# Local attention in six layers: the mask added by VectorE, the maximum taken off by GpSimd, and the second pair of query/key products moved ahead of the output product

## The chip, the cores and the metric

The kernel runs on one core of a Trainium2 chip. The metric is the device time of one execution in microseconds (us), measured outside the profiler; the profile is a separate look at one execution with its own time. The engines are TensorE (PE for matmuls, PEld for its weight loads), VectorE (DVE), ScalarE (ACT), GpSimd (POOL) and SyncE (SP), which issues the transfers. Each engine works through its own instructions in the order in which they stand, and semaphores tie the engines together.

## The reference, cut to what matters

The program has four parts and a last normalisation. The change is in the fourth, a network of six layers, each with a local attention and a feed-forward part, on 16 sequences of 256 tokens with 128 features. The attention has 16 heads of 64 features. A window is 32 tokens, and each token sees its own window and the one before, as far as the mask lets it.

```python
def local_attention(q, k, v):
    w = WINDOW                       # 32
    nw = n // w
    bk2, bv2 = (look(bk), look(bv))  # the window before, and the own one: 64 keys
    mask = (it < jb) | (it > jb + w) | (jb == -1)
    sim = jnp.einsum('bhwie,bhwje->bhwij', bq, bk2) * QK_SCALE
    sim = jnp.where(mask, -jnp.finfo(sim.dtype).max, sim)
    attn = jax.nn.softmax(sim, -1)
    out = jnp.einsum('bhwij,bhwje->bhwie', attn, bv2)
    return out.reshape(b, h, n, d)

def attn_layer(x, Wqkv, qs, ksc, Wo):
    q, k, v = jnp.split(x @ Wqkv, 3, -1)          # heads split off each
    q = l2norm(q) * qs
    k = l2norm(k) * ksc
    q = q * cos * scale + rotate_half(q) * sin * scale
    k = k * cos * inv + rotate_half(k) * sin * inv
    out = local_attention(q, k, v)
    return out @ Wo

for i in range(6):
    x = attn_layer(shift_tokens(x), ...) + x
    x = ffn_layer(shift_tokens(x), ...) + x
```

## The kernel before

**Tiling.** All layers run in `l1_network`, one loop over six layers. In a layer the 16 sequences follow each other, written out one by one; `N` counts them. A sequence has 256 tokens, so two blocks of 128, `j` = 0 and 1. What one call of `attention` does for one sequence has two halves, one for each `j`, and the four compute engines each have their own `attention` function that writes out that engine's part.

**A pipeline over three sequences.** In half `j` of sequence `N` the engines work at three sequences at once:

- for `N+1`, the query/key products `project_qk(N+1, 4j..4j+3)`, four of 128x512, called c below; each is squared by ScalarE (`square`) and multiplied by the rotary tables by VectorE (`rotate`), and the two halves of the rotation are added by GpSimd (`add`). VectorE sums the squares per head (`sum_squares`), ScalarE makes inverse norms of them (`inverse_norms`), GpSimd multiplies by these (`norm`), TensorE transposes the result (`turn_qk`) and ScalarE copies it (`copy_qk`). The value products are `project_v`;
- for `N`, the mask products, the scores, the softmax, the transposes of the weights (`turn_weights`) and their copies (`copy_weights`), and the weighted sums of the values (`weigh`, half a step later);
- for `N-1` (or the block before), the transposes of the normed output (`turn_output`), their copies (`copy_output`), the output product (`output`), and its sum with the residual in `X` (`add_attention`, on VectorE).

A sequence that is first in its layer has no `N-1` part (`prev` is false), and the last has no `N+1` part (`nxt` is false).

**The softmax before.** `masks` writes the mask into the two score banks `pS` with one bfloat16 product of an identity with the mask for each; `scores` accumulates onto it with 64 small products (two passes each in float32, so 128 in the trace). VectorE takes the maxima of `pS` (`maxima`), subtracts them into `E`, ScalarE exponentiates `E` (`exps`), VectorE sums it (`sum_exps`) and makes reciprocals.

**Two banks in turn.** All other products and transposes of a half go in turn into the banks 2 and 3 of the PSUM tile `pp`, in the order of the list `SHARED`. A use waits until the use before the last one, which had the same bank, has been read. In half `j` the order is: two value products, two `turn_output`, the output product (called y), then four `turn_qk`. So the output product takes the bank of the first `turn_output`, the first `turn_qk` that of the second `turn_output`, and the second `turn_qk` that of the output product: it waits for `add_attention`, which reads that bank and increments `s_x`. The query/key products have the banks 0 and 1, in turn by c.

```python
    def bank(*use):
        kind, c, d = at[use][1]
        freed(kind, c, N + d)
        return at[use][0]
```

```python
    elif kind == "y":
        after(pe, s_x, 2 * N + c + 1)
```

There is no scheduler: the order on each engine is the order of the calls in its `attention` function.

## Time and profile before

| | us |
|---|---|
| median of 3 runs | 4645.14 (4640.55 to 4652.28) |
| the profiled execution's own time | 4643.52 |
| its span, first to last instruction | 4641.7 |
| PE busy | 4093.0 (88%) |
| DVE busy | 3365.0 (72%) |
| ACT busy | 2392.2 (52%) |
| POOL busy | 2163.8 (47%) |

The profiled execution lies 1.6 us under the median, and its span 1.8 us under its own time. The busy shares are means over stages that differ: the six layers lie between about 1,090 and 4,600 us, and in the attention of a layer the pattern repeats with each sequence, so one sequence in the trace tells of nearly all of that stage. The places in the trace that matter here are named by their time from the span's start.

### The profile page before, as it was taken

The page shows a single profiled execution, that of the slowest core. Times are in us where ns is not written, and L with a number is a line of the kernel's source. Part 1 is how long each engine was busy: PE and PEld are TensorE (multiplying, and loading weights), DVE is VectorE, ACT ScalarE, POOL GpSimd, SP SyncE. Part 2 cuts the span into 40 slices and gives each one's busy share as a digit, 9 for nine tenths or more (in the row PEclk, how much of TensorE's full clock was granted, in tenths as well). Part 3 has the DMA queues.
Part 4 walks back from the last instruction along what each step waited for, and adds up shares of the span by engine and source line. Part 5 has one row for each costly group of instructions (what it writes and reads, how often), then busy time and mean ns, then how long its engine had stood idle before and what let it go on. Part 6 is the DMA issues. An engine that isn't in the chain of part 4 may idle for free. (4 is left out here: it accounts for less than half of the span.)

```text
span 4641.7 us, 175927 instructions
## 1 busy us (share of the span) xinstructions
PE 4093.0 (88%) x68914; PEld 2806.2 (60%) x68915; DVE 3365.0 (72%) x7216; ACT 2392.2 (52%) x5386; POOL 2163.8 (47%) x2301
## 2 busy tenths in 40 slices
PE   7999749576999889998899989999889998899995
PEld 4566416454666656666566665666656666566663
DVE  4777450576888778887788877888778887788876
ACT  4666423123666546665366653666536665366651
POOL 2444300103566436664366643666436664366651
PEclk9999769798999999999999999999999999999998
DMA  1000003003333223332233322333223332223221
GB/s 41 5 5 3 1 21 98 8 0 85 66 71 66 47 65 70 66 68 49 65 70 64 71 48 65 67 67 69 50 65 66 68 68 51 64 64 71 62 57 43
DMA packets 478517, 249.52 MB, mean 54 GB/s; under 512 B 65782, under 2 KB 472516, under 8 KB 476740
## 3 DMA queue, kind: packets, MB, share of 16 engines
q1 hardware_dynamic: 477764, 238.93, 23.1%
q8 instruction: 539, 8.83, 0.8%
q14 instruction: 214, 1.75, 0.1%
HBM read 35.40 MB, written 4.19 MB: 9 GB/s over the span
## 5 line engine op out<-in xcount | busy, mean ns | idle before, releaser
L1921 POOL TENSOR_TENSOR n_pre<-n_tt 128x512 f32<-128x512 f32 x768 | 970.9, 1275 | 886.1 <-DVE n_tt L2394 886.1
L2394 DVE TENSOR_TENSOR n_tt<-n_pp,n_rot 128x1024 f32<-128x1024 f32 x768 | 922.2, 1220 | 378.6 <-ACT n_sq L2255 378.5
L1942 POOL TENSOR_TENSOR n_pre<-n_pre,n_rn 128x512 f32<-128x512 f32 x768 | 776.6, 1042 | 284.4 <-ACT n_rn L2263 284.4
L2021 PE MATMUL n_pp<-n_wqkv,n_xT 128*128 128x512 f32 x1536 | 787.9, 615 | 10.7 <-ACT n_xT L2250 10.4
L2255 ACT ACTIVATE n_sq<-n_pp 128x512 f32<-128x512 f32 x768 | 459.1, 598 | 595.5 <-PE n_pp L2021 584.7
L2401 DVE TENSOR_REDUCE n_ss<-n_sq 128x8 f32<-128x512 f32 x768 | 518.8, 676 | 0.0
L2275 ACT COPY n_qkT<-n_pp 128x512 f32<-128x512 f32 x768 | 436.6, 594 | 136.6 <-PE n_pp L2037 136.1
L2037 PE MATMUL n_pp<-ident,n_pre 128*128 128x128 f32 x3072 | 433.2, 274 | 19.7 <-POOL n_pre L1942 14.5
L2051 PE MATMUL n_pp<-n_wo,n_OT 128*128 128x128 f32 x3072 | 398.7, 283 | 58.1 <-ACT n_OT L2281 57.1
L2037 PEld LDWEIGHTS n_pp<-ident,n_pre 128*128 128x128 f32 x3072 | 360.3, 142 | 129.1 <-issue 125.4
L2051 PEld LDWEIGHTS n_pp<-n_wo,n_OT 128*128 128x128 f32 x3072 | 361.4, 193 | 103.6 <-ACT n_OT L2281 101.2
L2281 ACT COPY n_OT<-n_pp 128x512 f32<-128x512 f32 x384 | 206.5, 589 | 339.4 <-PE n_pp L2044 339.4
L2028 PE MATMUL n_pp<-n_wqkv,n_xT 128*128 128x512 f32 x768 | 366.3, 597 | 0.0
L2071 PEld LDWEIGHTS n_pS<-n_qkT 64*32 64x32 f32 x24576 | 254.6, 105 | 162.0 <-issue 161.8
L301 POOL TENSOR_TENSOR a_E<-a_E,a_ri 128x256 f32<-128x256 f32 (+1 forms) x256 | 211.4, 826 | 291.8 <-DVE a_ri L536 291.3
L2021 PEld LDWEIGHTS n_pp<-n_wqkv,n_xT 128*128 128x128 f32 x1536 | 250.7, 192 | 139.0 <-issue 111.3
L2096 PE MATMUL n_pW<-n_V,n_ET 64*32 64x64 f32 x12288 | 295.8, 225 | 28.5 <-issue 28.5
L2408 DVE TENSOR_REDUCE n_nm<-n_pS 128x8 f32<-128x512 f32 x384 | 247.3, 686 | 97.8 <-PE n_pS L2071 97.8
L2096 PEld LDWEIGHTS n_pW<-n_Vx,n_ET 64*32 64x32 f32 x12288 | 249.7, 105 | 106.7 <-issue 106.7
L2071 PE MATMUL n_pS<-n_qkT 64*32 64x64 f32 (+1 forms) x24576 | 287.7, 222 | 23.5 <-issue 23.5
L2096 PE MATMUL n_pW<-n_Vx,n_ET 64*32 64x64 f32 x12288 | 290.1, 225 | 16.5 <-issue 11.6
L2431 DVE TENSOR_TENSOR n_On<-n_pW,n_ri 128x512 f32<-128x512 f32 x384 | 246.2, 683 | 43.4 <-PE n_pW L2096 41.7
(246 smaller groups left out, 7016.9 us busy)
## 6 DMA issues: line engine op xcount, KB each, us to landing
n_V<-n_Vn SPq DMA_DIRECT2D x768, 128.0 KB, 2.6
n_Vx<-n_Vn SPq DMA_DIRECT2D x384, 128.0 KB, 2.5
n_Vx<-n_Vn SPq DMA_DIRECT2D x576, 64.0 KB, 2.2
n_wqkv<-in_L_ffn_Wqkv SPq DMA_DIRECT2D x6, 1536.0 KB, 6.7
e_w<-in_L_ffn_w SPq DMA_DIRECT2D x32, 256.0 KB, 3.0
n_fxs<-X SPq DMA_DIRECT2D x48, 127.0 KB
m_Y<-e_ye SPq DMA_DIRECT2D x64, 64.0 KB, 2.1
n_wo<-in_L_ffn_Wo SPq DMA_DIRECT2D x6, 512.0 KB, 7.3
```

The source lines that it names most:

```text
L1921: nc.gpsimd.tensor_tensor(d, s[0], s[1][:, :, ::-1, :], ALU.add).then_inc(s_add, 1)
L1942: nc.gpsimd.tensor_tensor(d, d, bcast(rn[:, j, t, 8 * half:8 * half + 8], 2, D), ALU.mult).then_inc(s_kn, 1)
L2021: nc.tensor.matmul(pp[:, c % 2, :], xT[:, j * P:(j + 1) * P], wqkv[:, t * I + 512 * half:t * I + 512 * half + 512], start=True, stop=True) ...
L2028: nc.tensor.matmul(pp[:, bank, :], xT[:, j * P:(j + 1) * P], wqkv[:, 2 * I + 512 * half:2 * I + 512 * half + 512], start=True, stop=True). ...
L2037: last = nc.tensor.transpose(pp[:, bank, g * P:(g + 1) * P], pre[:, j, t, o:o + P], ident[:, :])
L2051: last = nc.tensor.matmul(pp[:, bank, 0:C], OT[:, j, k % 2, k // 2, :], wo[:, k, :], start=(k == 0), stop=(k == I // P - 1))
L2071: last = nc.tensor.matmul(pS[W * w:W * w + W, e, i * 2 * W + o:(i + 1) * 2 * W], qkT[r:r + D, 0, i, q:q + W], qkT[r:r + D, 1, i, lo:q + W] ...
L2096: last = nc.tensor.matmul(pW[W * w:W * w + W, f, o:o + D], ET[r:r + D, e, c, W * w:W * w + W], v[r:r + D, u, m, o:o + D], start=True, stop ...
L2255: nc.scalar.activation(sq[:, c % 2, :], pp[:, c % 2, :], ACT.Square).then_inc(s_sq, 1)
L2275: nc.scalar.copy(qkT[:, t, 4 * half:4 * half + 4, j * P:(j + 1) * P], pp[:, bank, :].rearrange("p (g q) -> p g q", g=4)).then_inc(s_qkT, 1)
L2394: nc.vector.tensor_tensor(tt[:, c % 4, :, :].rearrange("p s (h d) -> p s h d", d=D), bcast(pp[:, c % 2, :].rearrange("p (h d) -> p h d", d ...
L2401: nc.vector.tensor_reduce(ss[:, j, t, 8 * half:8 * half + 8], sq[:, c % 2, :].rearrange("p (h d) -> p h d", d=D), AX.X, ALU.add).then_inc( ...
```

## The change

The parts of the change, all in the attention of the six layers:

- `masks` and its bfloat16 identity go. The scores start their banks themselves (`start=True`). For the first window of a sequence, which has no window before it, the product now takes its own 32 keys twice, so that all 64 places hold something; the mask puts the first 32 out.
- VectorE adds the mask while it moves the scores from `pS` to `E` (`mask_scores`), and takes the maxima of `E`.
- GpSimd takes the maxima off (`take_maximum`), in place in `E`, after the four `norm` of the half and ahead of its four `add`.
- TensorE makes the second pair of query/key products right after `turn_output`, ahead of the output product; before, they stood between and behind the `turn_qk`. The second `turn_qk` stands ahead of `turn_weights`.
- ScalarE squares the second pair ahead of `exps` (there are four buffers of squares now); VectorE rotates both ahead of `sum_exps`, and `sum_exps` stands ahead of `add_attention`.

```diff
             def attention(N, u, b, prev, nxt, nxt2):        # GpSimd
...
+                for j in range(2):
+                    if nxt or not j:
+                        clamp_squares(N + j, 1 - j)
+                        for r in range(4):
+                            norm(N + j, 1 - j, r)
+                    take_maximum(N, j)
+                    if nxt:
+                        for c in range(4 * j, 4 * j + 4):
+                            add(N + 1, c)
+                    elif not j:
+                        ff_start(layer[0])
...
+            def take_maximum(N, j):
+                for e in range(2):
+                    after(pool, s_max, 4 * N + 2 * j + e + 1)
+                    x = E[:, e, :].rearrange("p (i s) -> p i s", s=2 * W)
+                    nc.gpsimd.tensor_tensor(x, x, bcast(nm[:, j, e, :], 2, 2 * W), ALU.subtract
+                                            ).then_inc(s_sub, 1)
...
-                    masks(N, j)                              # TensorE
                     if j == 1:
+                        held(pe, s_held)
                         weigh(u, 0)
...
+                    after(pe, s_masked, 4 * N + 2 * j)
...
+                            if j == 0 and w == 0:
+                                keys = bcast(qkT[r:r + D, 1, i, 0:W], 1, 2)
+                            else:
+                                keys = qkT[r:r + D, 1, i, q - W:q + W]
...
+                    if nxt:
+                        project_qk(N + 1, 4 * j + 2)
+                        project_qk(N + 1, 4 * j + 3)
                     if prev:
                         output(N - 1, j, bank("y", j, -1))
                     d = j
                     if nxt or not d:
                         turn_qk(N + d, 4 - 4 * j, bank("turn", 4 - 4 * j, d))
+                        turn_qk(N + d, 5 - 4 * j, bank("turn", 5 - 4 * j, d))
                     turn_weights(N, j)
-                    if nxt or not d:
-                        turn_qk(N + d, 5 - 4 * j, bank("turn", 5 - 4 * j, d))
-                    if nxt:
-                        project_qk(N + 1, 4 * j + 2)
...
+            def mask_scores(N, j):                           # VectorE
+                after(dve, s_S, 4 * N + 2 * j + 2)
                 after(dve, s_ETp, 4 * N + 2 * j)
                 for e in range(2):
...
+                                            bcast(win[:, j, :], 1, 8), ALU.add).then_inc(s_masked, 1)
+                for e in range(2):
+                    after(dve, s_masked, 4 * N + 2 * j + e + 1)
+                    nc.vector.tensor_reduce(nm[:, j, e, :], E[:, e, :].rearrange("p (i s) -> p i s", s=2 * W),
+                                            AX.X, ALU.max).then_inc(s_max, 1)
...
-                    maxima(N, j)
+                    mask_scores(N, j)
                     if nxt:
                         sum_squares(N + 1, 4 * j + 1)
+                        rotate(N + 1, 4 * j + 2)
+                        rotate(N + 1, 4 * j + 3)
+                    sum_exps(N, j)
                     if prev:
                         add_attention(N - 1, b - 1, j, at["y", j, -1][0])
-                    sum_exps(N, j)
                     if nxt:
-                        for c in (4 * j + 2, 4 * j + 3):
-                            rotate(N + 1, c)
-                            sum_squares(N + 1, c)
+                        sum_squares(N + 1, 4 * j + 2)
+                        sum_squares(N + 1, 4 * j + 3)
```

**On TensorE**, in the half `j` = 0 of a sequence inside a layer, from the output product to the last `turn_qk`. L2051 is the output product, L2037 `turn_qk`, L2083 `turn_weights`, L2021 a query/key product. Before:

```order
L2051 MATMUL n_pp<-n_wo,n_OT 128x128 [waits n_outT_copied]
L2051 MATMUL n_pp<-n_wo,n_OT 128x128 x7
L2037 MATMUL n_pp<-ident,n_pre 128x128 [waits n_qk_normed,n_outT_copied]
L2037 MATMUL n_pp<-ident,n_pre 128x128 x3
L2083 MATMUL n_pW<-ident,n_E 128x128 [waits n_exped,n_output_normed]
...
L2037 MATMUL n_pp<-ident,n_pre 128x128 [waits n_qk_normed,n_attention_added]
L2037 MATMUL n_pp<-ident,n_pre 128x128 x3
L1809 REGISTER_ALU
L2021 MATMUL n_pp<-n_wqkv,n_xT 128x512 [waits n_xT_copied,n_rotary_products]
L2037 MATMUL n_pp<-ident,n_pre 128x128 [waits n_qk_normed,n_qkT_copied]
```

Now, with the same steps at L2054, L2040, L2078 and L2024:

```order
L2024 MATMUL n_pp<-n_wqkv,n_xT 128x512 [waits n_xT_copied,n_rotary_products]
L2054 MATMUL n_pp<-n_wo,n_OT 128x128 [waits n_outT_copied]
L2054 MATMUL n_pp<-n_wo,n_OT 128x128 x7
L2040 MATMUL n_pp<-ident,n_pre 128x128 [waits n_qk_normed,n_outT_copied]
L2040 MATMUL n_pp<-ident,n_pre 128x128 x3
L1807 ISA
L2040 MATMUL n_pp<-ident,n_pre 128x128 [waits n_qk_normed,n_attention_added]
L2040 MATMUL n_pp<-ident,n_pre 128x128 x3
L2078 MATMUL n_pW<-ident,n_E 128x128 [waits n_exped,n_output_normed]
```

The `turn_qk` that waits for `add_attention` stood behind `turn_weights`; it stands ahead of it now, right behind the output product and the first `turn_qk`.

**On VectorE**, in the same half, from the scores on. Before, with L2408 the maxima, L2413 the subtraction, L2401 a sum of squares, L2438 `add_attention`, L2420 and L2423 `sum_exps`, L2394 `rotate`:

```order
L2408 TENSOR_REDUCE n_nm<-n_pS 128x8 [waits n_scored]
L2408 TENSOR_REDUCE n_nm<-n_pS 128x8
L1809 REGISTER_ALU [waits n_weights_turned]
L2413 TENSOR_TENSOR n_E<-n_pS,n_nm 128x512 [waits n_maxed] x2
L2401 TENSOR_REDUCE n_ss<-n_sq 128x8 [waits n_norms_made]
L2438 TENSOR_TENSOR X<-n_pp,X 128x128 [waits n_y_made]
L2420 TENSOR_REDUCE n_rs<-n_E 128x8 [waits n_exped] x2
L2423 RECIPROCAL n_ri<-n_rs 128x16 [waits n_exps_summed]
L1809 REGISTER_ALU [waits n_rotary_added]
L2394 TENSOR_TENSOR n_tt<-n_pp,n_rot 128x1024 [waits n_squared]
```

Now, with the mask at L2400, the maxima at L2405 and `add_attention` at L2429:

```order
L2400 TENSOR_TENSOR n_E<-n_pS,n_win 128x512 [waits n_weights_turned,n_scored]
L2400 TENSOR_TENSOR n_E<-n_pS,n_win 128x512
L1807 REGISTER_ALU
L2405 TENSOR_REDUCE n_nm<-n_E 128x8 [waits n_scores_masked] x2
L2392 TENSOR_REDUCE n_ss<-n_sq 128x8 [waits n_norms_made]
L1807 REGISTER_ALU [waits n_rotary_added]
L2385 TENSOR_TENSOR n_tt<-n_pp,n_rot 128x1024 [waits n_squared]
L1807 REGISTER_ALU [waits n_rotary_added]
L2385 TENSOR_TENSOR n_tt<-n_pp,n_rot 128x1024 [waits n_squared]
L2411 TENSOR_REDUCE n_rs<-n_E 128x8 [waits n_exped] x2
L2414 RECIPROCAL n_ri<-n_rs 128x16 [waits n_exps_summed]
L2429 TENSOR_TENSOR X<-n_pp,X 128x128 [waits n_y_made]
```

`add_attention` was the second step behind the softmax pair; now the two rotations, both sums of exponentials and the reciprocal stand ahead of it.

## Rows read from the trace of the kernel before

**Rows 1.** Busy time in a stretch of one sequence (us): engines, granted PE clock, DMA.

```profile
1302.33:1332.33 30.00, 29.05 (x640) 20.55 (x639) 24.89 (x36) 18.97 (x39) 18.95 (x20) 1.00 0.32 69
```

**Rows 2.** Timeline of PE in that sequence: start us, us, line, tiles [idle before].

```profile
1302.33 0.25 PE L2096 MATMUL n_pW<-n_Vx,n_ET 64*32 64x64 f32 x2
...
1303.74 1.98 PE L2021 MATMUL n_pp<-n_wqkv,n_xT 128*128 128x512 f32 x4
1305.56 1.88 PE L2028 MATMUL n_pp<-n_wqkv,n_xT 128*128 128x512 f32 x4
1307.37 1.46 PE L2071 MATMUL n_pS<-n_qkT 64*32 64x32 f32 x128
1308.76 1.09 PE L2044 MATMUL n_pp<-ident,n_On 128*128 128x128 f32 x8
1310.15 2.05 PE L2051 MATMUL n_pp<-n_wo,n_OT 128*128 128x128 f32 x16 [0.29 <-ACT n_OT L2281]
1312.04 0.60 PE L2037 MATMUL n_pp<-ident,n_pre 128*128 128x128 f32 x4
1312.47 1.04 PE L2083 MATMUL n_pW<-ident,n_E 128*128 128x128 f32 x8
1313.35 0.60 PE L2037 MATMUL n_pp<-ident,n_pre 128*128 128x128 f32 x4
1313.79 1.02 PE L2021 MATMUL n_pp<-n_wqkv,n_xT 128*128 128x512 f32 x2
1314.65 1.04 PE L2037 MATMUL n_pp<-ident,n_pre 128*128 128x128 f32 x8
...
1316.38 0.59 PE L2059 MATMUL n_pS<-n_win,n_eye 128*128 128x512 bf16 x2
1316.90 0.25 PE L2096 MATMUL n_pW<-n_Vx,n_ET 64*32 64x64 f32 x2
...
1321.95 1.48 PE L2071 MATMUL n_pS<-n_qkT 64*32 64x64 f32 x128
...
1330.65 0.43 PE L2014 MATMUL n_pp<-ident,n_xs 128*128 128x128 f32 x2 [0.37 <-ACT n_qkT L2275]
```

**Rows 3.** Timeline of DVE in the first half of that sequence.

```profile
1305.56 2.35 DVE L2394 TENSOR_TENSOR n_tt<-n_pp,n_rot 128x1024 f32<-128x1024 f32 x2
1307.83 0.67 DVE L2401 TENSOR_REDUCE n_ss<-n_sq 128x8 f32<-128x512 f32 x1
1308.90 1.29 DVE L2408 TENSOR_REDUCE n_nm<-n_pS 128x8 f32<-128x512 f32 x2 [0.40 <-PE n_pS L2071]
1310.10 1.28 DVE L2413 TENSOR_TENSOR n_E<-n_pS,n_nm 128x512 f32<-128x512 f32 x2
1311.30 0.68 DVE L2401 TENSOR_REDUCE n_ss<-n_sq 128x8 f32<-128x512 f32 x1
1312.24 0.29 DVE L2438 TENSOR_TENSOR X<-n_pp,X 128x128 f32<-128x128 f32 x1 [0.27 <-PE n_pp L2051]
1312.45 1.27 DVE L2420 TENSOR_REDUCE n_rs<-n_E 128x8 f32<-128x512 f32 x2
1313.75 0.25 DVE L2423 RECIPROCAL n_ri<-n_rs 128x16 f32<-128x16 f32 x1
```

**Rows 4.** Timelines of ACT and POOL in that half.

```profile
1310.82 1.23 ACT L2286 ACTIVATE n_E<-n_E 128x512 f32<-128x512 f32 x2 [0.23 <-DVE n_E L2413]
...
1313.21 1.08 ACT L2291 COPY n_ET<-n_pW 128x512 f32<-128x512 f32 x2
...
1306.88 4.05 POOL L1942 TENSOR_TENSOR n_pre<-n_pre,n_rn 128x512 f32<-128x512 f32 x4 [1.08 <-ACT n_rn L2263]
```

**Rows 5.** Busy time in stretches that begin with a PE gap; one at half clock.

```profile
1126.70:1133.90 7.20, 5.03 (x66) 3.36 (x68) 5.83 (x11) 5.33 (x10) 4.51 (x5) 1.00 0.68 144
...
4528.00:4535.20 7.20, 4.98 (x11) 2.26 (x12) 3.49 (x8) 1.62 (x3) 0.00 (x0) 0.76 0.05 11
```

**Rows 6.** The same view, of the granted clock's fall after one such gap.

```profile
1595.20:1598.59 3.39, 3.39 (x17) 3.07 (x16) 2.03 (x4) 2.31 (x4) 0.00 (x0) 0.50 0.10 22
1592.00:1595.00 3.00, 0.98 (x45) 0.89 (x45) 0.50 (x2) 0.00 (x0) 0.00 (x0) 1.00 0.08 18
```

More of the change, by code:

```diff
@@ L1961, in attention @@
                     stage(N + 2, u, b + 2)
-                clamp_squares(N, 1)
-                for r in range(4):
-                    norm(N, 1, r)
-                if nxt:
-                    for c in range(4):
-                        add(N + 1, c)
-                    clamp_squares(N + 1, 0)
-                    for r in range(4):
-                        norm(N + 1, 0, r)
-                    for c in range(4, 8):
-                        add(N + 1, c)
-                else:
-                    ff_start(layer[0])
+                for j in range(2):
[9 more added lines that the diff above has]
+                        ff_start(layer[0])
             def ff_stage(M, g, p):
@@ L2053, in output @@
                 last.then_inc(s_y, 1)
-            def masks(N, j):
-                after(pe, s_sub, 4 * N + 2 * j)
-                for e in range(2):
-                    nc.tensor.matmul(pS[:, e, :].rearrange("p (i s) -> p i s", s=2 * W), eye[:, :],
-                                     bcast(win[:, j, :], 1, 8), start=True, stop=False, skip_group_check=True)
             def scores(j):
@@ L2137, in attention @@
                         weights_ready(pairs[0], N - 1, 1 - u, 1)
-                    if not nxt:
-                        after(pe, s_qkT, 8 * N + 4 * j + 4)
-                    masks(N, j)
                     if j == 1:
+                        held(pe, s_held)
                         weigh(u, 0)
                     elif prev:
+                        held(pe, s_held)
                         weigh(1 - u, 1)
@@ L2147, in attention @@
                         project_qk(N + 1, 4 * j + 1)
-                        after(pe, s_qkT, 8 * N + 4 * j + 4)
+                    after(pe, s_qkT, 8 * N + 4 * j + 4)
+                    after(pe, s_masked, 4 * N + 2 * j)
+                    if nxt:
                         project_v(N + 1, 2 * j, bank("v", 2 * j, 1))
                         project_v(N + 1, 2 * j + 1, bank("v", 2 * j + 1, 1))
+                    else:
+                        held(pe, s_held)
                     scores(j)
@@ L2252, in square @@
             def square(N, c):
-                after(act, s_ss, 8 * N + c - 1)
+                after(act, s_ss, 8 * N + c - 3)
                 after(act, s_qk, 8 * N + c + 1)
-                nc.scalar.activation(sq[:, c % 2, :], pp[:, c % 2, :], ACT.Square).then_inc(s_sq, 1)
+                nc.scalar.activation(sq[:, c % 4, :], pp[:, c % 2, :], ACT.Square).then_inc(s_sq, 1)
             def inverse_norms(N, j):
```

45 lines of the change are left out of this document (13 added, 32 removed).

## The prediction

> **What bounds the kernel now.** I read the whole span in stretches of 100 us first; inside the attention of a layer they all look alike, so the next view is one sequence, 30.00 us long [rows 1]: PE is busy for 29.05 of it at a clock of 1.00, DVE for 24.89, ACT and POOL for 19 each. Then PE's timeline of that sequence [rows 2]. It runs without a break but for three short stops: 0.29 us ahead of the output product in each half (the bank of the first `turn_output` is not yet copied) and 0.37 us ahead of `turn_x`. So here PE is the bound, and whatever PE no longer does or no longer waits for shortens the sequence, until a wait of PE takes its place. A half runs from one start of `weigh` to the next: 1302.33 to 1316.90, 14.57 us, and 15.43 us for the other, which holds `turn_x`. There are 16 sequences in each of six layers; 14 of the 16 have a neighbour on both sides.
>
> **The change part by part.** I take the half from 1302.33 and price each step by the distance from its start to the next start in [rows 2], since PE overlaps the end of one product with the next.
>
> *What goes.* The mask products: 1316.38 to 1316.90, 0.52 us a half, all on the path. The stop of 0.29 us ahead of the output product: with two query/key products in front of it (0.86 us each, 1313.79 to 1314.65), ScalarE has 1.7 us more to copy, so it goes. That is 0.81 us a half, 1.62 a sequence, if nothing else becomes late. The products for the first window grow from 32 to 64 columns; the scores of the other half, which are all of 64, take 1.48 against 1.46 us, so 0.02. The new `held` rows on PE are sequencer rows without work; I bound them by 0 and 0.1 us a half and take 0.
>
> *What moves work off or onto VectorE.* Two additions of the mask take the place of two subtractions, from the same PSUM tile and of the same shape (two in 1.20 us, 1310.10 to 1311.30 [rows 3]); the maxima read SBUF now (before two in 1.20 us from PSUM, 1308.90 to 1310.10; `sum_exps` reads E and takes 1.27 for two against 1.29). So nothing.
>
> *GpSimd's two subtractions.* The nearest row is the four `norm`: in place, float32, 128x512, second operand broadcast over 64: 4.05 us, 1.0 each [rows 4]. In the new half GpSimd has finished `norm` about 2.2 us behind the end of the scores (1310.93 against 1308.76), when the first maxima are there too; the subtractions end at 3.2 and 4.2, the exponentials (0.6 each) at 3.9 and 4.9. Their first reader is `turn_weights` or `sum_exps`, which by the next paragraph come at 6.0 or later. So they are hidden, with 1 us of room; at 1.28 us each still; from about 1.6 us each they would show.
>
> *The wait that decides.* The second `turn_qk` goes into the bank of the output product and therefore waits for `add_attention`. Before it stood behind `turn_weights` and started at 1313.35, 0.8 us after `add_attention` had ended (1312.24 + 0.29 [rows 3]). Now PE reaches it earlier, and VectorE reaches `add_attention` later. I count from the end of the scores, 1308.76.
>
> - PE: two `turn_output` 0.88 (eight transposes, priced like the eight of `turn_weights`, 1312.47 to 1313.35, since their own row holds the stop), two query/key products 1.72, output product 1.89, first `turn_qk` 0.43: PE stands at the second `turn_qk` at **4.92**.
> - VectorE starts 0.14 behind (1308.90), then masks 1.20, maxima 1.20, a sum of squares 0.60, two rotations 2.27 (1305.56 to 1307.83), two sums of exponentials with the step to the reciprocal 1.30 (1312.45 to 1313.75), reciprocal 0.25, `add_attention` 0.29: **7.25**, and some 0.05 until PE sees it (ScalarE saw a subtraction 0.04 after its end, 1310.82). Nothing in this chain waits: squares, products and exponentials are all earlier.
>
> So PE waits 7.30 - 4.92 = **2.4 us in each half**, where nothing waited; as PE's last transposes end some 0.17 us after their issue (1312.04 + 0.60 against 1312.47), the visible gap is about 2.2. What is queued behind it on PE is the rest of the half: `turn_qk`, `turn_weights` and, behind their copies, `weigh`, and with it the next half's norms. All engines then run with room to spare.
>
> *The new half.* `weigh` 1.41, two query/key products 1.82, two value products 1.81, scores 1.39, then 7.30 to the end of the wait, then `turn_qk` 0.44, `turn_weights` 0.88, two `turn_qk` 0.87 and about 0.1 until `weigh` has its copies (ScalarE copies the second `turn_qk` ahead of the two weight copies, 1.08 [rows 4]): **16.0** against 14.57. In the half with `turn_x`, PE waits about 0.6 us for the copy that frees its bank and then turns for 0.27 (1330.65 on): **16.95** against 15.43. A sequence takes 33.0 instead of 30.0. The first sequence of a layer has no output product to wait for and gains the masks and some of the stop, about 0.5; the last has no rotations, yet has to wait for GpSimd in both halves; I bound it by 0 and 3 and take 2. A layer: 14 x 3.0 - 0.5 + 2 = 43.5; six: **+261 us**.
>
> *The clock.* Gaps of this size on PE are in the trace at the ends and starts of layers: 20 gaps of 2.17 to 2.40 us behind 1,100 us, of which the first and the last stand in [rows 5]. After nine, as after the first, the granted clock stayed at 1.00; after eleven, as after the last, it fell to half, the lower of its two levels (1.2 instead of 2.4 GHz), which makes the mean of these 7 us 0.76. [rows 6] show one fall: PE busy for 0.98 of 3 us, then 3.39 us at 0.50. In 3.4 us at half clock PE does the work of 1.7; some 0.5 of that falls into waits for copies (those ahead of `weigh` and `turn_x`), so I take 1.2 us a fall, between 0.7 and 1.7. Of 29 waits a layer I let 16 (11 in 20) be followed by a fall: 16 x 6 x 1.2 = **+115 us**. The Trainium skill ("TensorE: Matmul & The Clock Gate", section "HAM oscillation — how this bites in real kernels") tells of a kernel whose matmuls wait for a transfer at every tile and whose clock is throttled anew at every one of them. By that, all 174 waits would bring a fall; the nine gaps without one speak against it.
>
> *Sum.* 4643.5 (the profiled execution, 1.6 under the median) + 261 + 115 = 5020.
>
> **The rivals.**
>
> *A, the clock holds.* All waits as above, no fall: 4643.5 + 261 = 4905. For it: nine of 20 gaps. Against it: eleven, and here the gap comes at ever other places in time, so that some must be like these.
>
> *B, a fall at every wait.* 174 falls at 1.2 are 209, so 5113; at 1.7 they are 296, so 5200. For it: all eleven gaps with a fall are of 2.2 us or more, as long as the one expected here. Against it: three of that length had none.
>
> *C, faster: the wait doesn't bind.* Then 0.81 us goes from each half and PE stays the bound: a sequence takes 28.4, of which DVE's 24.89 still fit; 15 x 6 x 1.62 = 146, so 4498. It decides at 4.92 us behind the scores: `add_attention` would have to end by then, so the two rotations (2.27) would have to stand behind it, or the bank be another. Against it: the new order shows `n_attention_added` at that very row, and the rotations ahead of it on VectorE. For it there would have to be a step that I misread.
>
> *D, it evens out.* If the wait were 0.8 us, gain and loss would cancel: 4645. VectorE's chain would have to be 1.6 us shorter than its rows say; nothing points there.
>
> **How the numbers follow.** Forecast (waits of 2.4 us, some falls) 0.78; A 0.07; B 0.06; C 0.06; D 0.03. The predicted time is the forecast's, 5020. Its unknowns: 0.7 to 1.7 us a fall on a third to two thirds of the waits gives 40 to 200, and the last sequence of a layer ±6 to ±12 over six layers, so 4940 to 5115; A lies at 4905. The range from 4900 to 5105 leaves out C, D, most of B and the forecast's ends. What a measurement of this kernel can tell from no change is about 0.3%, 14 us. Slower by more than that: forecast, A, B, 0.91; within it: D, 0.03; faster: C, 0.06.
>
> **What would show each step right or wrong.** In the profile after: no L2059 rows and no idle time ahead of the output product; a wait of the second `turn_qk` for DVE's X of about 2.2 us, in some 29 halves a layer; `take_maximum` at 1.0 us with its exponentials done before `sum_exps` begins; PE's busy share in the attention near 86%; a sequence of 33 us where the clock holds; and a granted clock under 1.00 in most stretches of 100 us. The prediction is wrong if PE shows no wait for X, if DVE's steps behind the scores take less than 6 us until X is added, or if the halves differ in length without a change of the clock.

## The result, and the profile after

The changed kernel takes 5137.71 us (median of 4 runs, 5127.55 to 5158.42) against 4647.47 us (4640.55 to 4652.28) for the kernel before in the same runs: a ratio of 1.1062, 95% interval 1.1019 to 1.1104, so 490 us slower. The forecast was 5020, the range 4900 to 5105. The direction and the wait that makes most of the loss came as forecast; the time is 33 us above the range.

From the page after: the span, busy time and share of the engines, one DMA queue (packets, MB, share), and two groups of instructions (busy us, mean ns of one, idle time ahead and what ended it).

```profile
span 5156.6 us, 176394 instructions
PE 4199.3 (81%) x68530; PEld 2940.4 (57%) x68531; DVE 3336.3 (65%) x7214; ACT 2428.0 (47%) x5386; POOL 2536.6 (49%) x2685
q8 instruction: 539, 8.83, 0.7%
L2040 PE MATMUL n_pp<-ident,n_pre 128*128 128x128 f32 x3072 | 504.5, 304 | 382.8 <-DVE X L2429 367.8
L1961 POOL TENSOR_TENSOR n_E<-n_E,n_nm 128x512 f32<-128x512 f32 x384 | 392.5, 1043 | 76.8 <-DVE n_nm L2405 73.2
```

PE is now busy for 81% of the span. The waits of PE say why: 174 waits of up to 2.2 us of `turn_qk` (L2040) for the residual's sum on DVE (L2429), 29 a layer, where the kernel before had none.

```profile
PE n_pp L2040 <- DVE X L2429: 367.8, 174, 2.2
PE n_pW L2091 <- issue: 123.1, 89, 2.7
```

The second row has a sister in the view of the waits of the kernel before, where `weigh` is L2096; it stands in none of the rows ahead of the prediction, and that is where the prediction fell short:

```profile
PE n_pW L2096 <- issue: 40.1, 65, 1.2
```

One half of a sequence on PE's timeline after (start, us, line; idle time and its releaser in brackets), to be laid beside [rows 2]. It is the half with `turn_x` (L2017), from one start of `weigh` to the next, 1302.86 to 1319.74:

```profile
1309.31 1.09 PE L2047 MATMUL n_pp<-ident,n_On 128*128 128x128 f32 x8
1310.24 1.88 PE L2024 MATMUL n_pp<-n_wqkv,n_xT 128*128 128x512 f32 x4
1311.96 1.95 PE L2054 MATMUL n_pp<-n_wo,n_OT 128*128 128x128 f32 x16
1313.74 0.60 PE L2040 MATMUL n_pp<-ident,n_pre 128*128 128x128 f32 x4
1316.45 0.66 PE L2040 MATMUL n_pp<-ident,n_pre 128*128 128x128 f32 x4 [2.10 <-DVE X L2429]
1316.94 1.04 PE L2078 MATMUL n_pW<-ident,n_E 128*128 128x128 f32 x8
1317.81 1.04 PE L2040 MATMUL n_pp<-ident,n_pre 128*128 128x128 f32 x8
1319.38 0.43 PE L2017 MATMUL n_pp<-ident,n_xs 128*128 128x128 f32 x2 [0.53 <-ACT n_qkT L2270]
1319.74 0.25 PE L2091 MATMUL n_pW<-n_Vx,n_ET 64*32 64x64 f32 x2
...
1322.95 0.24 PE L2091 MATMUL n_pW<-n_Vx,n_ET 64*32 64x64 f32 x2 [1.79 <-issue]
1323.19 1.98 PE L2024 MATMUL n_pp<-n_wqkv,n_xT 128*128 128x512 f32 x4
```

There are two breaks. The first, of 2.10 us, is the forecast wait. The forecast has no term for the second: `weigh` starts at 1319.74, runs for about a microsecond and stops; what ends the stop is "issue", so no semaphore of the profile. "Stop" below is such a break in the dense products of `weigh`; its length is counted from the start of the last product ahead of it to the start of the next, here 1320.93 to 1322.95. DVE's timeline in the same half, the chain that PE waits for, beside [rows 3]:

```profile
1309.44 1.29 DVE L2400 TENSOR_TENSOR n_E<-n_pS,n_win 128x512 f32<-128x512 f32 x2 [0.44 <-PE n_pS L2068]
1310.65 1.27 DVE L2405 TENSOR_REDUCE n_nm<-n_E 128x8 f32<-128x512 f32 x2
1311.84 0.68 DVE L2392 TENSOR_REDUCE n_ss<-n_sq 128x8 f32<-128x512 f32 x1
1312.43 2.35 DVE L2385 TENSOR_TENSOR n_tt<-n_pp,n_rot 128x1024 f32<-128x1024 f32 x2
1314.69 1.27 DVE L2411 TENSOR_REDUCE n_rs<-n_E 128x8 f32<-128x512 f32 x2
1315.99 0.25 DVE L2414 RECIPROCAL n_ri<-n_rs 128x16 f32<-128x16 f32 x1
1316.16 0.23 DVE L2429 TENSOR_TENSOR X<-n_pp,X 128x128 f32<-128x128 f32 x1
```

And the windows (PE, PEld, DVE, ACT, POOL busy, granted clock, DMA share, GB/s): a half with nothing but the wait, the next half with a stop and a fall of the clock, the 3 us ahead of that fall, and the fall (a stretch at a granted clock of 0.50).

```profile
1302.86:1319.74 16.88, 14.25 (x318) 10.28 (x318) 12.33 (x18) 9.91 (x20) 11.57 (x12) 1.00 0.26 57
1319.74:1339.45 19.71, 15.73 (x317) 11.84 (x316) 12.33 (x18) 9.54 (x19) 11.26 (x11) 0.91 0.26 56
1332.70:1335.70 3.00, 0.81 (x8) 0.57 (x6) 2.97 (x6) 1.01 (x2) 3.00 (x3) 1.00 0.75 157
1335.70:1339.11 3.41, 3.41 (x18) 3.41 (x17) 0.88 (x2) 1.82 (x4) 1.93 (x3) 0.50 0.11 29
```

**Where the 490 us are.** I cut both traces at the starts of `weigh` and took the 168 halves that have a neighbour on both sides (28 a layer). Their mean went from 15.27 to 17.99 us: +457. A sequence without a stop or the start of a fall went from 29.96 to 33.45 us (the means of its two halves, 15.39 + 14.58 and 17.09 + 16.36): 84 x 3.49 = +293. 90 of the halves hold a fall of the clock, none did before; each adds 1.23 us (0.36 us for each us at half clock, as a line through all halves gives it, times 3.41): +111. The stops inside `weigh` sum to 103.8 against 45.7 us: +58. That makes 462, 5 too many, since these parts overlap a little. Outside these halves, the first half of each layer took 16.5 us more in all, and the ends and starts of the layers 18: +34. (The two profiled executions lie 515 us apart, more than the medians; the other 24 us lie ahead of the layers, where the change does nothing.)

The +293 is not the wait alone. In the changed kernel PE also stops on "issue" in the scores and right behind them, in 21 of the 168 halves for 18.6 us in all; before, in none of these halves (the twelve of L2071 lie at the ends of the layers). The waits after, and in the third row those of the scores before:

```profile
PE n_pS L2068 <- issue: 33.0, 24, 2.4
PE n_pp L2047 <- issue: 10.7, 11, 1.7
PE n_pS L2071 <- issue: 23.5, 12, 2.4
```

Without these halves, and without those into which a fall of the half before reaches, a sequence takes 33.11 us.

Of the 92 falls (two halves hold two), 74 begin between 0.2 us before and 1.2 us after the end of the wait for X; the other 18 begin 2 to 5 us behind a start of `weigh`, right behind a stop.

**What a stop is.** Ahead of each of them a transfer of 16 KB on the instruction queue q8 begins, 2.3 to 2.7 us before PE goes on in the changed kernel. The DMA view of the stretch 1320.00 to 1321.50 (busy tenths in 40 slices, and the one queue that moved anything) shows it for the stop above:

```profile
DMA  0000000000000009000000000000000000000000
q8 instruction: 1, 0.02, 3.9%
```

The sixteenth slice begins at 1320.56, 0.8 us behind the start of `weigh`; PE goes on at 1322.95, 2.4 us later. In all kernels of this study PE goes on 2.40 to 2.56 us after such a transfer began (mean of each kernel's stops) and the stop begins 1.1 us behind the start of `weigh`; what differs is when the transfer begins. There are 40 to 61 stops in the 168 halves of each kernel, 53 in the one before, where they were 0.83 us long. A transfer alone makes no stop: each half has two or three of them, and most halves have no stop. In the changed kernel all 48 stops of these halves fall on the same eight halves of every layer. That PE waits for these transfers is read from their times; no run takes the transfers away.

### The profile page after: what moved, and what is told of

Read it like the earlier page. It is cut to its first block and busy times, and to the rows that moved or that the text cites. A ratio compares the mean times of both kernels' runs of the same rounds, so it can differ in the third digit from the quotient of the medians.

```text
span 5156.6 us, 176394 instructions
## 1 busy us (share of the span) xinstructions
PE 4199.3 (81%) x68530; PEld 2940.4 (57%) x68531; DVE 3336.3 (65%) x7214; ACT 2428.0 (47%) x5386; POOL 2536.6 (49%) x2685
## 5 line engine op out<-in xcount | busy, mean ns | idle before, releaser
L1919 POOL TENSOR_TENSOR n_pre<-n_tt 128x512 f32<-128x512 f32 x768 | 954.2, 1275 | 135.3 <-DVE n_tt L2385 135.3
L2385 DVE TENSOR_TENSOR n_tt<-n_pp,n_rot 128x1024 f32<-128x1024 f32 x768 | 906.9, 1218 | 110.5 <-ACT n_sq L2250 110.1
L2040 PE MATMUL n_pp<-ident,n_pre 128*128 128x128 f32 x3072 | 504.5, 304 | 382.8 <-DVE X L2429 367.8
L2024 PE MATMUL n_pp<-n_wqkv,n_xT 128*128 128x512 f32 x1536 | 788.7, 636 | 12.7 <-ACT n_xT L2245 12.7
L2040 PEld LDWEIGHTS n_pp<-ident,n_pre 128*128 128x128 f32 x3072 | 404.8, 158 | 442.4 <-DVE X L2429 409.2
L2392 DVE TENSOR_REDUCE n_ss<-n_sq 128x8 f32<-128x512 f32 x768 | 503.0, 674 | 0.0
L2054 PEld LDWEIGHTS n_pp<-n_wo,n_OT 128*128 128x128 f32 x3072 | 374.4, 193 | 98.6 <-issue 79.1
L1961 POOL TENSOR_TENSOR n_E<-n_E,n_nm 128x512 f32<-128x512 f32 x384 | 392.5, 1043 | 76.8 <-DVE n_nm L2405 73.2
L2024 PEld LDWEIGHTS n_pp<-n_wqkv,n_xT 128*128 128x128 f32 x1536 | 274.8, 199 | 236.5 <-issue 212.2
L2054 PE MATMUL n_pp<-n_wo,n_OT 128*128 128x128 f32 x3072 | 379.6, 277 | 13.7 <-ACT n_OT L2276 13.6
L2400 DVE TENSOR_TENSOR n_E<-n_pS,n_win 128x512 f32<-128x512 f32 x384 | 247.5, 686 | 138.3 <-PE n_pS L2068 138.3
L2068 PE MATMUL n_pS<-n_qkT 64*32 64x64 f32 x24576 | 291.5, 226 | 33.0 <-issue 33.0
```

Source lines behind the costliest of these rows:

```text
L1919: nc.gpsimd.tensor_tensor(d, s[0], s[1][:, :, ::-1, :], ALU.add).then_inc(s_add, 1)
L1961: nc.gpsimd.tensor_tensor(x, x, bcast(nm[:, j, e, :], 2, 2 * W), ALU.subtract).then_inc(s_sub, 1)
L2024: nc.tensor.matmul(pp[:, c % 2, :], xT[:, j * P:(j + 1) * P], wqkv[:, t * I + 512 * half:t * I + 512 * half + 512], start=True, stop=True) ...
L2040: last = nc.tensor.transpose(pp[:, bank, g * P:(g + 1) * P], pre[:, j, t, o:o + P], ident[:, :])
L2054: last = nc.tensor.matmul(pp[:, bank, 0:C], OT[:, j, k % 2, k // 2, :], wo[:, k, :], start=(k == 0), stop=(k == I // P - 1))
L2068: last = nc.tensor.matmul(pS[W * w:W * w + W, e, i * 2 * W:(i + 1) * 2 * W], qkT[r:r + D, 0, i, q:q + W], keys, start=True, stop=True)
```

## The experiments

All ratios are to the kernel before in the same runs, with 95% intervals. Four things had to be told apart: the wait for the residual's sum, the clock, the stops inside `weigh`, and the share of the mask's move.

### The wait: the sum between the rotations

```diff
                         rotate(N + 1, 4 * j + 2)
+                    if prev:
+                        add_attention(N - 1, b - 1, j, at["y", j, -1][0])
+                    if nxt:
                         rotate(N + 1, 4 * j + 3)
                     sum_exps(N, j)
-                    if prev:
-                        add_attention(N - 1, b - 1, j, at["y", j, -1][0])
```

> The changed kernel with one step moved on VectorE: the sum with the residual (add_attention) stands between the two rotations, not behind both and behind the sums of exponentials. If the wait of the second turn_qk for that sum is what the change costs (theory W): the output product ends 4.5 us behind the scores, the sum 0.3 later, PE reaches that turn_qk at 4.9, so the wait and most falls of the clock go; 0.8 us a half against the kernel before remain as a gain, less the longer stops inside weigh (some 75 us in the changed kernel's trace), so 4540 to 4640. If the subtraction on GpSimd lengthens the softmax (theory G): the time stays near the changed kernel's, above 4900. If the stops inside weigh bring the falls of the clock (theory S): the wait goes, the stops of 2.2 us stay, with some 50 falls of 1.2 us: 4600 to 4700.

4703.54 us, ratio 1.0111 (1.0077 to 1.0145). Moving one call of 0.23 us on DVE takes some 440 us off the changed kernel (1.1062 - 1.0111, times 4650). The time lies above the 4540 to 4640 that theory W gave. The wait for X is gone from PE's waits, and what now stands first is the stop:

```profile
PE n_pW L2091 <- issue: 141.5, 104, 2.7
```

A sequence without stop or fall takes 29.01 us, 0.95 less than before (the parts that go promised 1.6). And still the kernel is 1.1% slower than before: the stops sum to 117 us in the 168 halves, and 23 falls come with them, all in halves with a stop.

### The stops: slow work ahead of `weigh`

The changed kernel, with one product of 128x512 (0.87 us), whose result nothing reads, right ahead of `weigh`:

```diff
+                    if j == 1 or prev:
+                        held(pe, s_held)
+                        after(pe, s_masked, 4 * N + 2 * j)
+                        nc.tensor.matmul(pS[:, 0, :], ident[:, :], wo[:, 0:4, :].rearrange("p k n -> p (k n)"),
+                                         start=True, stop=True)
                     if j == 1:
-                        held(pe, s_held)
                         weigh(u, 0)
                     elif prev:
-                        held(pe, s_held)
                         weigh(1 - u, 1)
```

> The changed kernel with one product more in each half, right ahead of weigh: a float32 product of the identity with 512 columns of Wo into a score bank that the scores overwrite; its result is not used, and it is about 0.87 us of PE. In the changed kernel weigh stops about 64 times for 2.1 us on average in its last quarter, in the kernel before, with a product and the masks (1.4 us) ahead of weigh, for 0.8 us. If PE's instructions come too late there (theory S) and slow work ahead of weigh gives them time: the stops shrink by about 0.9 us, to 1.3, 75 us in place of 132; falls of the clock become rarer, perhaps by a third (40 us). Against that stand 190 products, 165 us if all are on the path. So 5137 + 165 - 57 - 40 = 5200, and 5160 to 5250. If the stops have another cause, they keep their 2.1 us: 5300. The wait for the residual's sum stays at 2.1 us in both.

5189.79 us, ratio 1.1154 (1.1113 to 1.1195). Added work of 0.87 us in each of 186 halves would be 162 us; the kernel grew by 43. The wait for X is untouched, the stops went from a mean of 2.22 us to 1.17, and the falls from 90 to 63:

```profile
PE n_pp L2040 <- DVE X L2432: 369.7, 174, 2.2
PE n_pW L2091 <- issue: 49.3, 49, 1.7
```

A sequence without stop or fall grew by 1.65 us, so the added work is on the path, and most of what it costs comes back from stops and falls. The length of a stop hangs on what PE does right ahead of `weigh`.

### The two parts of the change alone

First the mask and GpSimd's part alone, with the products, squares, rotations and transposes in the old order:

```diff
-                    if nxt:
-                        project_qk(N + 1, 4 * j + 2)
-                        project_qk(N + 1, 4 * j + 3)
                     if prev:
                         output(N - 1, j, bank("y", j, -1))
...
+                    turn_weights(N, j)
+                    if nxt or not d:
                         turn_qk(N + d, 5 - 4 * j, bank("turn", 5 - 4 * j, d))
-                    turn_weights(N, j)
+                    if nxt:
+                        project_qk(N + 1, 4 * j + 2)
...
+                    if nxt:
+                        project_qk(N + 1, 4 * j + 3)
```

> One part alone: the mask added by VectorE and the maximum taken off by GpSimd as in the changed kernel; the second pair of query/key products, its squares, rotations, the second turn_qk and add_attention stand where the kernel before has them. Theory W: no wait for the residual's sum. But turn_weights, 3.5 us behind the scores, now comes ahead of the exponentials, which end 3.9 and 4.9 us behind the scores because of GpSimd: some 1.1 us of wait a half in two pieces, less 0.5 for the masks: 31.1 us a sequence against 30.0, and with longer stops in weigh 4760 to 4840. Theory G: the subtraction costs as much as the whole change, above 5000. If the mask part is a plain gain (its chain hidden): 4550.

4790.75 us, ratio 1.0293 (1.0257 to 1.033). No fall in the 168 halves; the stops have a mean of 1.32 us, with the product (0.86) ahead of `weigh` but not the masks (0.52). Most of the loss is a wait of `turn_weights` for the exponentials, which in this order come later than PE, behind GpSimd's two subtractions (276 times, 12 before). The second row, ahead of the output product, stood at 57.1 us before:

```profile
PE n_pW L2078 <- ACT n_E L2283: 118.0, 276, 3.4
PE n_pp L2054 <- ACT n_OT L2278: 62.4, 183, 1.4
```

Then the moves alone, with the mask products and DVE's subtraction as before (the diff is that of the change without `mask_scores`, `take_maximum` and the scores' own start):

> The other part alone: the second pair of query/key products ahead of the output product, squares, rotations, both first turn_qk ahead of turn_weights, the sums of exponentials ahead of add_attention, all as in the changed kernel; mask products on PE, maxima and subtraction on VectorE as before. Theory W: VectorE's chain ahead of add_attention has the same length as in the changed kernel, 7.25 us, so the turn_qk waits its 2.1 us in every half; with the masks (0.5 us a half) a sequence takes 34.1 us: 4985 without a fall of the clock, up to 5150 with a fall at every second wait. The stops in weigh, with 0.5 us of mask products ahead, lie between those of the kernel before and of the changed one. Theory G: about the kernel before or faster, 4550 to 4660.

5101.36 us, ratio 1.0963 (1.0926 to 1.1001). The wait is there at nearly its full size, 70 falls with it, and with the masks alone ahead of `weigh` the stops have 1.56 us:

```profile
PE n_pp L2037 <- DVE X L2434: 354.7, 170, 2.1
```

The moves thus hold most of the loss.

### The clock: the wait filled with work

Two products more in each half, read by nothing, right where PE waits for X:

```diff
                         turn_qk(N + d, 4 - 4 * j, bank("turn", 4 - 4 * j, d))
+                        if prev:
+                            after(pe, s_masked, 4 * N + 2 * j + 2)
+                            for e in range(2):
+                                nc.tensor.matmul(pS[:, e, :], ident[:, :],
+                                                 wo[:, 4 * e:4 * e + 4, :].rearrange("p k n -> p (k n)"),
+                                                 start=True, stop=True)
                         turn_qk(N + d, 5 - 4 * j, bank("turn", 5 - 4 * j, d))
```

> The changed kernel with two products more in each half, whose results nothing reads (identity by 512 columns of the output weights, 0.87 us each, into pS), right ahead of the second turn_qk, where TensorE waits 2.2 us for add_attention. They take 1.74 us of that wait and change nothing that the wait is for. If the clock falls of the changed kernel come from this gap: they drop from 90 to under 30 and the time by 70 to 110 us, to 5030 to 5070 us, while the wait for VectorE's add_attention drops from 367.8 to some 70 us without any gain of its own. If the falls come from the stops inside weigh: they stay at 80 to 90 and the time at 5120 to 5180 us.

5039.68 us, ratio 1.0862 (1.0824 to 1.09): with 1.74 us of work added to each half the kernel is faster than the changed one, by 0.0200 x 4634 = 93 us. The falls in the 168 halves go from 90 to 25, all of these in halves with a stop, 3 to 6 us behind the start of `weigh`; 65 falls of 1.23 us are 80 us, and the stops gave another 11 us (93.2 against 103.8). A sequence without stop or fall still takes 33.40 us, since X is as late as before:

```profile
PE n_pp L2040 <- DVE X L2435: 70.1, 165, 0.6
```

This run parts the two prices of the wait: the lost time itself, and the clock that an idle PE loses.

### A bank of its own for the output product

`pS` is empty once `mask_scores` has read it, so the output product can go there and no transpose waits for its sum. DVE's order stays that of the changed kernel; PE waits for the sum ahead of the next use of `pS` instead.

```diff
-    SHARED = ([..., ("o", 2, -1), ("o", 3, -1), ("y", 0, -1)] + [("turn", 4 + r, 0) for r in range(4)]
-              + [..., ("o", 0, 0), ("o", 1, 0), ("y", 1, -1)]
+    SHARED = ([..., ("o", 2, -1), ("o", 3, -1)] + [("turn", 4 + r, 0) for r in range(4)]
+              + [..., ("o", 0, 0), ("o", 1, 0)]
...
-                        output(N - 1, j, bank("y", j, -1))
+                        after(pe, s_masked, 4 * N + 2 * j + 2)
+                        output(N - 1, j, None)          # None: pS[:, 0, 0:C]
```

> The changed kernel, but the output product writes into pS, which mask_scores has emptied by then, instead of a bank of pp shared with the transposes; VectorE's order is untouched, so add_attention still comes after two rotations and the sums. Theory W (the wait was for the bank alone): the wait of turn_qk on VectorE's add_attention is gone from the waits (367.8 us in the changed kernel, under 10 here), a sequence takes 28.4 to 29.1 us as in e1_add_between, and the time is 4680 to 4730 us, stops of TensorE inside weigh staying at 2.2 to 2.4 us each, some 60 of them. Rival (the late sum holds up something else, the scores that need pS again or the residual): the wait turns up at another line and the time stays above 4850 us.

4670.23 us, ratio 1.0057 (1.0035 to 1.0079). The time is a little under the range expected. The wait for X is gone though the sum is as late as ever (7.3 us behind the start of the last score product in both kernels); it was the bank alone that made it matter. A sequence without stop or fall takes 28.74 us; stops of 2.33 us, 26 falls:

```profile
PE n_pW L2092 <- issue: 126.9, 60, 2.7
```

### Cover for the stops, three ways

The last product of a half back ahead of `weigh`, on top of the own bank; its square, rotation and sum of squares go to the end of the half with it, so the sum with the residual stands behind one rotation instead of two and ahead of the sums of exponentials. TensorE's part:

```diff
                         project_qk(N + 1, 4 * j + 2)
-                        project_qk(N + 1, 4 * j + 3)
...
+                    if nxt:
+                        project_qk(N + 1, 4 * j + 3)
                     if j == 1 and nxt2:
                         turn_x(N + 2, u, bank("x", 0, 2))
```

> e8_own_bank with the last of the four q/k products of a half (0.86 us) put back right ahead of weigh and its square, rotation and sum of squares at the end of VectorE's and ScalarE's half. Theory S (a stop inside weigh is as long as the slow TensorE work right ahead of weigh leaves it: 0.83 us with 1.4 us of it, 1.2 to 1.3 with 0.87, 2.2 to 2.4 with none): stops of 1.1 to 1.3 us, some 60 of them, the sequence as in e8 or 0.1 us longer, so 66 us less than e1_add_between's 4704 from the stops and up to 28 from its 23 falls: 4600 to 4650 us, level with the kernel before or just under it. Rival (the stops come from somewhere else and stay at 2.3 us): 4700 to 4730 us.

4607.75 us, ratio 0.9928 (0.9904 to 0.9953): the first that is faster than before, in the range expected. But the stops only shrank to 1.95 us, not to 1.1 to 1.3, and 21 falls stayed. Of the gain on e8_own_bank, 33 us are in the sequence without either (28.35 us), 13 in the stops and some 14 in the falls of the 168 halves, and 24 in the first halves of the layers, where the six falls went and the stops sum to 2.2 us instead of 14.1. The expectation got the time in part for a wrong reason.

The output product itself, 1.9 us, ahead of `weigh`; one value product takes its old place, and the sum with the residual goes to the end of VectorE's half:

```diff
+                    if prev:
+                        after(pe, s_masked, 4 * N + 2 * j + 2)
+                        output(N - 1, j, None)
                 if not nxt:
```

> The output product (8 matmuls, 1.9 us) goes right ahead of weigh, into pS as in e8; one v product of a half goes behind the scores to fill its old place, inverse norms ahead of the first squares on ScalarE, and add_attention last in VectorE's half. All four q/k products stay early. Theory S: with 1.9 us or more of slow work ahead of weigh the stops shrink to under 0.5 us each; against that a sequence takes some 0.9 us more than e8's, because the copies of v hold the transposes' bank and the waits for the exponentials add to some 0.4 us a half: 29.3 to 29.8 us against 30.0 in the kernel before, whose stops add 46 us: 4560 to 4620 us, a little under the kernel before. Rival (stops not covered, 2.3 us x 60): 4690 to 4760 us.

4677.47 us, ratio 1.0083 (1.0058 to 1.0107), where 4560 to 4620 was expected. The sequence came out as expected (29.54 us), the stops did not: 1.43 us, with twice the slow work of e2_extra_product ahead and a longer stop. That the length of the slow work decides (theory S) fails on these two runs. In both the stops with `turn_x` right ahead are the longer ones: 2.09 against 1.86 us in e9_bank_late_product, 1.64 against 1.30 in e10_late_output. `turn_x` needs a bank that ScalarE has to free: in e9_bank_late_product it does so at some 1271.5 us, 0.6 ahead of `weigh`, whatever stands before, though PE's timeline shows no idle time there:

```profile
1271.73 0.43 PE L2017 MATMUL n_pp<-ident,n_xs 128*128 128x128 f32 x2
1272.10 0.25 PE L2092 MATMUL n_pW<-n_Vx,n_ET 64*32 64x64 f32 x2
...
1275.27 0.24 PE L2092 MATMUL n_pW<-n_Vx,n_ET 64*32 64x64 f32 x2 [1.76 <-issue]
```

So theory L: what counts is how long before `weigh` the last thing that PE must wait for came. To try it, `turn_x` too gets a place in `pS`, and with that no bank to wait for:

```diff
-              + [("turn", r, 1) for r in range(4)] + [("x", 0, 2)])
+              + [("turn", r, 1) for r in range(4)])
...
-                        turn_x(N + 2, u, bank("x", 0, 2))
+                        after(pe, s_masked, 4 * N + 4)
+                        turn_x(N + 2, u, None)          # None: pS[:, 1, 0:T]
```

> e9_bank_late_product, where turn_x too writes into pS (its second half) instead of a bank shared with turn_qk, so that in the second half of a sequence nothing that TensorE waits for stands between the late product and weigh. Theory L (what shortens a stop inside weigh is not the slow work ahead of it as such, but how long before weigh the last wait ahead of it ended): in e9 the second halves' stops were 2.09 us although the product stood ahead, because turn_x waited there for ScalarE's copies until weigh's start; here they fall to 1.3 to 1.7 us while those of the first halves stay at 1.8 to 1.9: 10 to 20 us off the stops and up to 15 off the falls that come with them, 4575 to 4600 us, ratio to before 0.986 to 0.992. Theory S (the slow work ahead alone): turn_x and the product are there as before, the second halves' stops stay at 2.1 us and the ratio at e9's 0.993.

4553.31 us, ratio 0.9822 (0.98 to 0.9845): 1.8% faster than the kernel before and 11% faster than the changed one, beyond the range expected. (The expectation says that `turn_x` waited until the start of `weigh`; the rows above show 0.6 us less.) The stops ahead of which `turn_x` stands fell from 2.09 to 1.59 us, within what was expected, the others from 1.86 to 1.76; there are 4 falls instead of 21, and the sequence without either takes 28.08 us. PE's share of the span is that of the kernel before again, at a shorter span:

```profile
PE 4018.3 (88%) x68530; PEld 2790.5 (61%) x68531; DVE 3323.5 (73%) x7214; ACT 2360.6 (52%) x5386; POOL 2548.3 (56%) x2685
```

And the stops in PE's waits:

```profile
PE n_pW L2093 <- issue: 88.2, 58, 2.4
```

Its gain on e9_bank_late_product in the 168 halves is 64 us: 22 from the shorter sequence, 14 from the stops, 28 from the falls.

All stops side by side, each row a mean over all of one kernel's stops, the ends of the layers too (the start of the 16 KB transfer counted from the start of `weigh`):

| kernel | ahead of `weigh` on PE | stops | mean us | transfer starts | falls in 168 halves |
|---|---|---|---|---|---|
| before | product 0.86, masks 0.52 | 65 | 0.83 | -0.57 | 0 |
| e2_extra_product | unread product 0.87 | 52 | 1.17 | -0.19 | 63 |
| e4_mask_alone | product 0.86 | 56 | 1.32 | -0.06 | 0 |
| e10_late_output | output product 1.9 | 71 | 1.43 | -0.04 | 6 |
| e5_moves_alone | masks 0.52 | 62 | 1.56 | 0.18 | 70 |
| e11_x_own_bank | product 0.86, no bank to wait for | 60 | 1.69 | 0.38 | 4 |
| e9_bank_late_product | product 0.86, in half of them a bank to wait for | 59 | 1.95 | 0.63 | 21 |
| e12_fill_wait | transposes behind waits | 60 | 2.03 | 0.71 | 25 |
| after | transposes behind waits | 59 | 2.22 | 0.86 | 90 |
| e8_own_bank | transposes behind waits | 60 | 2.33 | 1.03 | 26 |
| e1_add_between | transposes behind waits | 62 | 2.38 | 0.95 | 23 |

The mean stop follows the start of the transfer in all rows but the last two, as it must where PE goes on a nearly fixed time after that start; the table does not say why a transfer begins when it does. That slow work ahead of `weigh` shortens the stop is shown by the first two experiments on it; that something to wait for behind that work takes the cover away fits e9_bank_late_product and e11_x_own_bank, but the latter's 1.69 us against 1.32 in e4_mask_alone with the same product, and e10's 1.43, are not accounted for to the tenth. What exactly sets the start of a transfer stays open.

## Why the prediction was wrong, point by point

**What bounds, what goes, GpSimd.** Right, but for what the masks and products had covered (see the sum). The masks and the stop ahead of the output product are gone, PE is the bound up to the new wait. GpSimd's subtraction takes 1.04 us against 1.0 from [rows 4], and the exponentials, by ScalarE's timeline in the half shown, end 0.6 us before `sum_exps` begins, so it is hidden here; e4_mask_alone shows what it costs where its cover is gone.

**The wait that decides.** Right in place, count and size. DVE's chain from the end of the scores to the end of the sum was 7.1 us (1309.31 to 1316.39), forecast 7.25; PE stood at the second `turn_qk` some 4.9 us behind the scores, forecast 4.92; the visible gap was 2.1 us on the mean (1.6 to 2.2) in 174 halves, forecast 2.2 in 29 a layer. The half shown has 16.88 us, forecast 16.95; the mean of all halves without stop or fall is 0.14 above that, and 0.36 above the 16.0 of the other half. That is 3.49 us a sequence instead of 3.0, 41 us in all. But the 33.11 us that are left when the halves with a stop in or behind the scores and those lengthened by an earlier fall are taken out lie 0.1 above the forecast 33.0: the price of the wait itself was right. That the wait is the cause of most of the loss is shown from both sides: e1_add_between took the late sum away, e8_own_bank the bank, and they took 440 and 466 us off (for the latter 1.1062 - 1.0057, times 4640).

**The clock.** Right in size, and in number partly by luck: 90 halves with a fall, of 1.23 us each, in the 168, forecast 96 of 1.2 in 174. e12_fill_wait shows that most come from the wait, but 18 of the 92 falls came right behind a stop, which the forecast did not know. Rival B, a fall at every wait, is refuted by the same count. The Trainium skill ("TensorE: Matmul & The Clock Gate", section "HAM oscillation — how this bites in real kernels") has the clock throttled anew at each wait of its kernel, whose waits are longer than these, so it says less of a wait of 2.2 us than the prediction took from it; here 47 of the 120 halves with the wait and no stop had a fall.

**The sum: the step that failed.** It has no term for the stops inside `weigh`. In the paragraph on the new half, `weigh` is put at 1.41 us, and under "What goes" the masks are all gain, as are the products that move forward. But the masks and the late product of [rows 2] were what PE had to do right ahead of `weigh`, and while it did it, an instruction transfer was under way. The row of 40.1 us on `issue` in the waits of before said that every third half stopped there already, with that cover; the one sequence that I read, [rows 1, 2], happened to hold none. I took away 1.38 us of cover and priced it at nothing. The stops more than doubled, from 45.7 to 103.8 us in the 168 halves: 58 us, half of what the time was above the forecast, and the largest of the parts that the sum missed. With the 18.6 us of stops in and behind the scores and the 10 us more in the first halves of the layers, stops that the sum put at nothing account for up to 86 of the 118 us. Why PE now stops at the scores too is not shown. A half with a stop also nearly always had a fall: 43 of 48.

**The ends of the layers: mis-sized.** The first sequence of a layer was to gain 0.5 us and the last to lose 2; the ends together measured +34 us over six layers where the sum had 9. The first half of a layer alone lost 2.75 us, 16.5 in all, and that is the same step again: each of the six holds a stop in `weigh` (14.6 us in all, 5.0 before) and a fall, where before none did. In e9_bank_late_product, without those falls and with 2.2 us of stops, the six take 87.9 us, against 110.1 in the changed kernel and 93.6 before. What the other 18 us are stays open.

**The range.** Sequences 41, stops 58, ends 25, less 4 on the falls and the 5 of overlap: 115 more than the 376 of the sum, which is the measured 490 to 1 us. Its unknowns were the falls, which came out as taken, and the last sequences; the stops were no unknown of it at all, since they were not seen.

## What to carry to other kernels

Work that is moved away from in front of a dense run of small instructions may have hidden a stop there: look for waits on "issue" in the whole trace, not in one clean period, before booking it as gain. A product that takes a bank in turn makes everything that follows in that bank wait for its reader; a bank of its own removes the wait without touching the reader's order. And an idle stretch of PE has two prices, its length and the clock after it, which can be told apart by filling it with work that nothing reads.

## What the runs showed of the hardware

PE stops in the middle of 64 small products for up to 2.7 us, with nothing to wait for in the profile, and a transfer of 16 KB on the instruction queue had begun 2.40 to 2.56 us before it went on (mean of each kernel). With 1.4 us of slow work ahead of `weigh` the transfers began 0.57 us before its start and the stops were 0.83 us long; with none, 0.7 to 1.0 us behind its start, and 2.0 to 2.4 us long.

Added work made the program faster: two unread products of 1.74 us a half, put into a wait, took off 93 us, mostly because the granted clock fell in 25 halves and not in 90.

Short stops cost little or no clock: in the 168 halves of the kernels without the wait for X, stops with a mean of 0.83 and 1.32 us had no fall, 1.43 and 1.69 us had 6 and 4, 1.95 us had 21, and 2.33 and 2.38 us had 26 and 23.
